# Attention and expert kernel on one core: last down groups reordered, gates by half rows, first half's results spread

## The reference, cut to what matters

```python
xn = _layernorm(x)
q, k, v = xn @ Wq.T + bq, xn @ Wk.T + bk, xn @ Wv.T + bv
phi_q, phi_k = elu(q) + 1, elu(k) + 1
s = (phi_q * cumsum(phi_k * v, axis=1) * SCALE) @ Wo.T + bo
h = gelu(buf @ w1.T + b1) @ w2.T + b2          # buf: the tokens in their slots
g = silu(gathered h * prob)
out = x + s * g
```

## Time and profile before

| | us |
|---|---|
| median of 3 runs | 2147.61 |
| lowest, highest | 2146.22, 2152.90 |
| the profiled execution's own time | 2152.81 |
| its span, first to last instruction | 2150.7 |
| PE busy | 2001.0 |
| DVE busy | 1380.1 |
| ACT busy | 687.4 |
| POOL busy | 471.6 |
| mean granted TensorE clock | 0.971 of full speed |

### The profile page before, as it was taken

The page is one execution under the profiler, slowest core; times in us unless marked ns, Lnnn a source line. Parts: engine busy times, 40 slices in busy tenths (PEclk is TensorE's granted clock), DMA queues, the critical chain, the costliest instruction groups (busy, mean ns, idle before and its releaser), DMA issues.

```text
span 2150.7 us, 27040 instructions
## 1 busy us (share of the span) xinstructions
PE 2001.0 (93%) x9380; PEld 910.8 (42%) x9380; DVE 1380.1 (64%) x2074; ACT 687.4 (32%) x1087; POOL 471.6 (22%) x577
## 2 busy tenths in 40 slices
PE   7799999999658999999999999989999999999993
PEld 2244454554223444444444443434444444444441
DVE  3587888778549766677667766476454544455453
ACT  1222222223335434443453343333122212221221
POOL 0078888888750000000000000110000000000002
PEclk9799999999879999999999999999999999999997
DMA  8566766667888776767676676874533333333334
GB/s 279 217 212 231 229 230 215 227 229 216 250 205 328 254 258 222 266 206 240 226 248 212 223 247 226 284 214 128 176 98 105 104 101 103 98 106 101 98 117 78
DMA packets 180278, 419.87 MB, mean 195 GB/s; under 512 B 17808, under 2 KB 74704, under 8 KB 178384
## 3 DMA queue, kind: packets, MB, share of 16 engines
q1 hardware_dynamic: 143728, 292.65, 41.9%
q0 software_dynamic: 29024, 117.51, 17.1%
q10 hardware_dynamic: 7424, 8.39, 1.3%
HBM read 268.51 MB, written 166.77 MB: 202 GB/s over the span
## 4 chain that ended last, share of the span: by engine, by line
PE 61%; POOL 13%; DMA 11%; DVE 6%; issue 4%; ACT 3%; another core or an unknown queue 1%; ACTq 0%; SPq 0%; DVEq 0%; POOLq 0%
PE pair L1761 33%; PE pair L1723 26%; DMA arena<-w_down 3%; DMA arena<-w_up 3%; DMA arena<-x_t 2%; PE pair L1577 2%; POOL arena L702 1%; POOL arena L704 1%; POOL arena L679 1%; POOL arena L691 1%; POOL arena L693 1%; POOL arena L695 1%; POOL arena L706 1%; POOL arena L696 1%; DMA arena<-up_sums 1%
## 5 line engine op out<-in xcount | busy, mean ns | idle before, releaser
L1761 PE MATMUL pair<-arena 128*128 128x512 f16 x3360 | 731.9, 380 | 7.7 <-DVE arena L1450 5.0
L1723 PE MATMUL pair<-xnT,arena 128*128 128x512 f16 x2400 | 537.4, 384 | 28.8 <-ACT arena L913 14.4
L1761 PEld LDWEIGHTS pair<-arena 128*128 128x128 f16 x3360 | 329.0, 98 | 407.7 <-issue 14.3
L1450 DVE SCALAR_TENSOR_TENSOR arena<-pair,arena 128x1024 f32<-128x1024 f32 x248 | 303.0, 1223 | 189.6 <-PE pair L1761 189.2
L1645 PE MATMUL pair<-arena 128*128 128x512 f16 x1728 | 385.9, 381 | 12.1 <-DVE xnT L423 12.1
L1723 PEld LDWEIGHTS pair<-xnT,arena 128*128 128x128 f16 x2400 | 236.5, 99 | 323.2 <-issue 20.7
L932 ACT ACTIVATE arena<-arena 128x512 f16<-128x512 f32 x280 | 170.2, 626 | 582.4 <-PE pair L1761 516.6
L1645 PEld LDWEIGHTS pair<-arena 128*128 128x128 f16 x1728 | 169.1, 98 | 208.6 <-issue 19.6
L1723 PE MATMUL pair<-xnT 128*128 128x512 f16 x960 | 216.6, 382 | 17.6 <-ACT xnT L863 17.6
L1426 DVE SCALAR_TENSOR_TENSOR arena<-arena 128x512 f16<-128x512 f32 x280 | 188.8, 683 | 10.9 <-ACT arena L932 9.1
L1723 PEld LDWEIGHTS pair<-xnT 128*128 128x128 f16 x960 | 94.4, 99 | 133.7 <-ACT xnT L863 18.6
(11 more groups left out here) (190 smaller groups left out, 1753.5 us busy)
## 6 DMA issues: line engine op xcount, KB each, us to landing
down_dram<-arena SPq DMA_DIRECT2D x70, 512.0 KB, 4.3
arena<-down_dram SPq DMA_DIRECT2D x70, 512.0 KB, 3.3
up_dram<-arena SPq DMA_DIRECT2D x100, 256.0 KB
arena<-up_dram SPq DMA_DIRECT2D x100, 256.0 KB, 2.6
arena<-w_up POOLq DMA_DIRECT2D x40, 512.0 KB, 5.3
up_sums<-arena POOLq DMA_DIRECT2D x40, 512.0 KB, 3.7
arena<-w_down POOLq DMA_DIRECT2D x40, 512.0 KB, 5.2
down_sums<-arena POOLq DMA_DIRECT2D x40, 512.0 KB, 3.6
```

What stands on the lines that cost most here:

```text
L1450: ins = nc.vector.scalar_tensor_tensor(to, src, scale, to, ALU.mult, ALU.add)
L1723: ins = mm(out_to, w[:, a, c * P:(c + 1) * P], x_in_op[:, b, c, :], start=(first and i == 0), stop=(i == 11), skip_group_check=True)
L1761: ins = mm(bank[2 + h][:, (t % 2) * BLOCK:(t % 2 + 1) * BLOCK], g_ops[:, A_NAMES.index(name), c, a, t * P:(t + 1) * P], down_ring[:, j, c, ...
```

## The change

LAST is the second half's last down group (n = 19). There PE does the tiles in two passes: all seven products for tiles 0 and 1, then all seven for tiles 2 and 3. DVE adds each tile by itself (`last_add`, 128x512), and PE waits before each tile for the last add to the same bank half. ACT gates each block of a tile by itself (`last_gate`, 128x512) in the order LAST_GATES, C11, C12, C22, C21 for the tiles of a pass. The results are made in the order 0, 1, 4, 5, 2, 3, 6, 7 within the down group, between adds, and POOL stores them in that order (LAST_TILES). In both halves' last down group only S3, S2 and the low part of S2 stand ahead of the first add; S4, S1 and the other low parts follow between the adds. The first half's results are spread: in quads 20 and 21 one is made after `p167`, one after `c22`, one after `c21` and one after `context(k, 3)`.

```diff
@@ -397,6 +397,18 @@
             return k // 2 - 1, (4, 5, 6) if 0 < k < 2 * GROUPS else ()
         VALUES = ("11", "22", "12", "21")
+        LAST = STEPS - 1
+        def last_at(j, t):
+            return 14 * LAST + 14 * (t // 2) + 2 * j + t % 2
+        LAST_INTO = {C11: 1, C12: 4, C22: 5, C21: 6}
+        LAST_GATES = [(c, 2 * h + t) for h in range(2) for c in (C11, C12, C22, C21) for t in range(2)]
+        LAST_TILES = (0, 1, 4, 5, 2, 3, 6, 7)
         def chain_bank(k):
             return out_bank(k % 2)
@@ -747,7 +759,7 @@
             def add_rows(half, i):
                 st = HALF_TILES * half + i
-                pool.wait_ge(fin_ready, st + 1)
+                pool.wait_ge(fin_ready, HALF_TILES + LAST_TILES.index(i) + 1 if half else i + 1)
                 pool.indirect_dma_start(
                     out, bass.IndirectOffsetOnAxis(ap=meta_s[:, st, 0:1].bitcast(U32), axis=0), fs(i, half), None,
                     bounds_check=TOKENS - 1, oob_is_err=False, compute_op=ALU.add).then_inc(fin_stored[i % PAIRS], 16)
@@ -757,7 +769,7 @@
             for half in range(HALVES):
                 if half:
                     save_s(GROUPS + ATT_GROUPS - 1)
-                for i in range(HALF_TILES):
+                for i in LAST_TILES if half else range(HALF_TILES):
                     add_rows(half, i)
             for i in range(PAIRS):
                 pool.wait_ge(fin_stored[i], 64)
@@ -932,13 +944,17 @@
                 nc.scalar.activation(g_ops[:, A_NAMES.index(name), k % 2, HI, :], g_block(name), ACT.Copy,
                                      scale=CS if is_attention(n) else HS).then_inc(g_hi, 1)
-            def gate(half, i):
-                st = HALF_TILES * half + i
+            def gate(i):
                 act.wait_ge(meta_loaded, 16)
-                act.wait_ge(down_added, 14 * (GROUPS * (half + 1) - 1) + (14 if i >= PAIRS else 10))
+                act.wait_ge(down_added, 14 * (GROUPS - 1) + (14 if i >= PAIRS else 10))
                 row = acc[:, i % PAIRS, 2 * (i // PAIRS):2 * (i // PAIRS) + 2, :].rearrange("p c e -> p (c e)")
-                nc.scalar.activation(row, row, ACT.Silu, scale=meta_s[:, st, 1:2].bitcast(F32)).then_inc(gate_ready, 1)
+                nc.scalar.activation(row, row, ACT.Silu, scale=meta_s[:, i, 1:2].bitcast(F32)).then_inc(gate_ready, 1)
+            def last_gate(c, t):
+                st = HALF_TILES + PAIRS * (c // 2) + t
+                act.wait_ge(down_added, last_at(LAST_INTO[c], t) + 1)
+                nc.scalar.activation(acc[:, t, c, :], acc[:, t, c, :], ACT.Silu, scale=meta_s[:, st, 1:2].bitcast(F32))\
+                  .then_inc(gate_ready, 1)
             def gate_weights():
                 act.wait_ge(scaled, 1)
...
-                gate(1, i)
+            for c, t in LAST_GATES:
+                last_gate(c, t)
@@ -1450,9 +1466,19 @@
                     ins = nc.vector.scalar_tensor_tensor(to, src, scale, to, ALU.mult, ALU.add)
                 ins.then_inc(down_added, 1)
+            def last_add(j, t):
+                dve.wait_ge(down_done, 14 * LAST + last_at(j, t) + 1)
+                dve.wait_ge(down_added, last_at(j, t) - 1 if j else 14 * LAST)
+                to = acc[:, t, DOWN_INTO[j], :]
+                nc.vector.scalar_tensor_tensor(to, bank[2 + t // 2][:, (t % 2) * BLOCK:(t % 2 + 1) * BLOCK], 1.0 / (HS * WM),
+                                               to, ALU.mult, ALU.add).then_inc(down_added, 1)
             def result(half, i):
-                st = HALF_TILES * half + i
-                dve.wait_ge(gate_ready, st + 1)
+                if half:
+                    dve.wait_ge(gate_ready, HALF_TILES + LAST_GATES.index((C21 if i >= PAIRS else C12, i % PAIRS)) + 1)
+                else:
+                    dve.wait_ge(gate_ready, i + 1)
                 dve.wait_ge(fs_loaded[i], 16 * (half + 1))
                 row = acc[:, i % PAIRS, 2 * (i // PAIRS):2 * (i // PAIRS) + 2, :].rearrange("p c e -> p (c e)")
                 nc.vector.tensor_tensor(fs(i, half), fs(i, half), row, ALU.mult).then_inc(fin_ready, 1)
...
                 p167(k)
-                if half and k in (2 * GROUPS, 2 * GROUPS + 1):
-                    for i in range(PAIRS):
-                        result(0, i + PAIRS * (k % 2))
+                finishing = half and k in (2 * GROUPS, 2 * GROUPS + 1)
+                if finishing:
+                    result(0, PAIRS * (k % 2))
                 if ups:
                     low_up(k + 1, 2)
                 for j in downs[:-3]:
...
                 c22(k)
+                if finishing:
+                    result(0, PAIRS * (k % 2) + 1)
                 for j in downs[-3:-2]:
                     low_down(m, j)
                 context(k, 1)
                 if ups:
                     low_up(k + 1, 4)
                 c21(k)
+                if finishing:
+                    result(0, PAIRS * (k % 2) + 2)
                 if in_line(k):
                     low_g(k, "22")
                 for j in downs[-2:-1]:
...
                 context(k, 3)
+                if finishing:
+                    result(0, PAIRS * (k % 2) + 3)
                 if in_line(k):
                     low_g(k, "12")
                 for j in downs[-1:]:
@@ -1516,14 +1548,6 @@
                 last = n % GROUPS == GROUPS - 1
                 k = 2 * n + 2
                 ups = half == 0 and not last
-                if last:
-                    e = 2 * n + 1
-                    s3(e)
-                    s2(e)
-                    s4(e)
-                    s1(e)
-                    for name in ("S2", "S1", "S4", "S3"):
-                        low_g(e, name)
                 for j in range(7):
                     add_down(n, j, 0)
                     if j and not last:
@@ -1535,15 +1559,35 @@
                     if j == 0 and not last:
                         s3(k)
                         s2(k)
-                    if last and j == 6 and half:
-                        for i in range(PAIRS):
-                            result(half, i)
                     if ups:
                         low_up(2 * n + 3, j)
                         for i in downs_under(n).get(j, ()):
                             low_down(n + 1, i)
                 if not last:
                     low_g(k, DOWN_A[6])
+            def last_down(n):
+                half, e = n // GROUPS, 2 * n + 1
+                s3(e)
+                s2(e)
+                low_g(e, "S2")
+                for at in range(14):
+                    if half:
+                        j, h = at % 7, at // 7
+                        last_add(j, 2 * h)
+                        last_add(j, 2 * h + 1)
+                    else:
+                        j, h = at // 2, at % 2
+                        add_down(n, j, h)
+                    if at == 0:
+                        s4(e)
+                        s1(e)
+                    elif at < 4:
+                        low_g(e, ("S1", "S4", "S3")[at - 1])
+                    if half:
+                        for i in {5: (0,), 6: (1,), 7: (4,), 8: (5,), 11: (2,), 12: (3,), 13: (6, 7)}.get(at, ()):
+                            result(half, i)
             for half in range(HALVES):
                 n0 = half * GROUPS
...
                 for n in range(n0, n0 + GROUPS):
                     if n < n0 + GROUPS - 1:
                         quad(2 * n + 2)
-                    down(n)
-                    if n < n0 + GROUPS - 1:
+                        down(n)
                         quad(2 * n + 3)
-            for i in range(PAIRS, HALF_TILES):
-                result(1, i)
+                    else:
+                        last_down(n)
@@ -1746,23 +1789,35 @@
                 pe.wait_ge(copy_ready, 3 * k + 3)
                 product(k, 6, chain, False)
+            def down_tile(n, j, t):
+                i = 0
+                for c in range(2):
+                    for a, b in PASSES:
+                        ins = mm(bank[2 + t // 2][:, (t % 2) * BLOCK:(t % 2 + 1) * BLOCK],
+                                 g_ops[:, A_NAMES.index(DOWN_A[j]), c, a, t * P:(t + 1) * P], down_ring[:, j, c, b, :],
+                                 start=(DOWN_STARTS[j] and i == 0), stop=(i == 5), skip_group_check=True)
+                        i += 1
+                ins.then_inc(down_done, 1)
             def down(n):
                 for j in range(7):
-                    name = DOWN_A[j]
                     pe.wait_ge(down_w[j], 16 * (n + 1))
-                    pe.wait_ge(g_lo, made_count(2 * n + 1, name))
+                    pe.wait_ge(g_lo, made_count(2 * n + 1, DOWN_A[j]))
                     for t in range(PAIRS):
-                        h, e = t // 2, 14 * n + 2 * j + t // 2
+                        e = 14 * n + 2 * j + t // 2
                         if t % 2 == 0 and e >= 2:
                             pe.wait_ge(down_added, e - 1)
-                        i = 0
-                        for c in range(2):
```

(20 more changed lines are left out.)

7 lines of the change are left out of this document (3 added, 4 removed).

## The result

| | before | changed |
|---|---|---|
| median, us | 2147.53 (4 runs, 2146.22 to 2152.90) | 2122.99 (4 runs, 2119.28 to 2131.61) |
| ratio | | 0.9890, 95% interval 0.9862 to 0.9918 |
| profiled execution, us | 2152.81 | 2131.61 |
| its span, us | 2150.7 | 2129.8 |

The change saves 24.5 us by the medians, where 32.9 were forecast. The prediction said 2115 us, with a range of 2107 to 2128; the measured 2123 lies in it. Each of the two profiled executions is the slowest of its four.

The account below looks back on a forecast made before the run. Bounds: PE, busy 93% of the span, and 35.7 us behind the last matmul, bound by transfers. Savings 5.4 + 10 + 0.3 - 0.6 + 17.8 = 32.9 us gave 2115 us from the median, range 2107 to 2128.

Parts of the forecast that it names:

- rival 1: Quads' feed (kv rows, s_dram rows, SP's late up loads) replaces the results as limit: 3 instead of 10 us, 2122; chance 0.2.
- The tail: Behind the last matmul: most stores move beside matmuls, span ends 17.9 us after it instead of 35.7, 17.8 saved.
- the quads: Quads 20 to 22: spreading the first half's results removes idle and slow starts, about 10 us saved, bounds 3 and 13.
- First half's last down group: Only S2's low half stays ahead of the first add: idle 0.9 instead of 3.36 us, 5.4 saved in all.
- the slow start: First half's last down group: 14 matmuls behind the idle at 0.427 instead of 0.216 us, 2.95 us counted as saved.
- The steps up to quad 21's fifth product: Quad 20 onward: 0.9 us idle left of 4.16, fifth product at 1402.4 instead of 1407.2, 4.8 us gained.
- Margin 3 to 5 us less a landing of about 4: this may cost 0 to 3: Quad 22's first product: SP issues up loads only after rows 4 to 7; possible cost 0 to 3 us, within bounds.
- two of the prediction's own signs of being wrong: Quads 21 and 22: SP's up loads releasing PE or DVE waits over 2 us; granted clock of 0.50.
- Second half's last down group: Two passes of tiles: idle 1.35 instead of 1.65 us, 0.3 saved, less 0.6 for the turns.
- the turns: Second half's last down group: each tile added while PE does the other, 0.4 us spare; cost 0.6 us, bounds 0 and 2.
- Rivals 2 and 3: Second half's last down: turns cost 8.4 us, 2122.5, chance 0.07; matmuls blocked by DVE reading the bank pair, 2174, chance 0.03.
- Rival 4: Tail: first tiles' stores wait until the second pass is over, about 9 of 17.8 us lost, 2124; chance 0.05.

Follow-up runs that it names:

- e4: Changed kernel with all four sums and four low parts again ahead of the first add in the first half's last down group: 2126.79 us.
- e6: The kernel before the change, run and profiled again without any edit: 2128.71 us, ratio 0.9997 to the runs beside it.
- e2: Changed kernel with quad 22's up operands 0 to 3 each loaded ahead of the wait for store 0 to 3: 2120.01 us.
- e8: e2 with the first half's results 4 to 7 made later, 4 behind quad 21's C21, 5 to 7 in quad 22: 2098.00 us.
- e3: Changed kernel with the second half's last down group by pairs of tiles again, all results behind the last add: 33.8 us behind the last matmul.
- e10: The changed kernel again, unedited, timed beside the kernel before: 2109.03 us against 2133.34, ratio 0.9891.
- e1: Changed kernel with the first half's results again in a row behind P1+P6+P7 in quads 20 and 21: 2128.71 us.
- e9: e8 with GpSimd's 32 scatters issued after the first down group: 2088.53 us against 2133.34 for the kernel before, ratio 0.9794.
- e7: Changed kernel with GpSimd's 32 scatters issued after the first down group: 2098.13 us against 2127.72 for the kernel before, ratio 0.9860.

## Why the prediction was right, and where it was not

The forecast saving was 32.9 us, the measured one 24.5, and rival 1's number, 2122, is nearer to 2123 than the forecast's 2115. The tail was forecast well; the quads were not, and the number lies in the range because the range takes in rival 1.

*First half's last down group.* 0.9 us of idle was forecast, 0.83 measured; the 5.4 us are (a) before less (a) after. But 2.95 of these are the slow start, and this was read from one execution as if it were steady. e4 and e6 have the same idle without it. Against those two this edit saves 2.5 us.

*Quads.* The steps up to quad 21's fifth product hold: idle 0.9 forecast, 0.76 measured; at that product 1402.4 was forecast, 4.8 gained, and 7.3 measured (from C11 of quad 20, 32.0 against 24.7), since context 3 did not wait for its kv rows at all: they are issued 3.4 us earlier after C11 than before (10.3 against 13.7) and are there within 7.1 us instead of 12.0. That stop is not steady either: e6, with its results in a row, has none. The round-robin rule (the Trainium skill, DMA: Bandwidth & Descriptors, section SWDGE vs HWDGE vs iDMA) was drawn on for rival 1: a kv load would not get shorter as long as any store is in flight. The trace does not bear out what was drawn from it, since two stores were issued around this load (1386.79 and 1389.01).

The step that failed is "Margin 3 to 5 us less a landing of about 4: this may cost 0 to 3". SP was free 31.0 us after quad 20's C11 (before 30.5), as forecast. But PE came to quad 22's first product at 32.7, where 34.8 was forecast and 39.8 measured before, so the margin was 1.7 us, not 3 to 5; and the landing took 8.2 us, not 4. The cost was 6.7 us of idle and 2.8 of slow start. So the quads gave 4.6 instead of 10. I had the right wait in the sum, with a price near the 3.8 us of the same load in the kernel before (5.1 in e6), and no fall of the clock behind it. In the kernel before no store was issued between 1391.30 and 1412.36; in the changed one a store goes out at 1406.65, 1.2 us before this load, and it took 8.2, 8.0 and 9.3 us in the three traces of the changed kernel. The other six up loads also follow it more closely here (within 5.1 us against 10.1), so which of the two made it slow is not shown. e2 shows the cause of the wait, and e8 what lay behind it. Rival 1 named SP's late up loads, and two of the prediction's own signs of being wrong are in the trace, an up load that releases PE after more than 2 us and a clock of 0.50 behind it: here the rival took place.

*Second half's last down group.* Forecast: idle 1.35 instead of 1.65 and 0.6 for the turns, +0.3 in all; measured: idle 1.18, (d) 38.3 against 38.2. The turns cost about 0.8 us (38.3 less 36.3 of matmuls and 1.2 of idle). Rivals 2 and 3 are out: 156 matmuls in 34.37 us, 0.220 each. What I did not see is that the sums' new places alone would have taken all idle there (e3).

*Tail.* T + 17.9 forecast, T + 17.8 measured; before T + 35.7, so 17.9 saved against the first profile and 16.4 against e6. Last store at T + 4.8 forecast, 4.7 measured. The store landed 6.6 us later, at T + 11.3, where 11.8 was forecast, and from there to the end are 6.5 us, not 6.1: two small misses that offset each other. Rival 4 is out. The Trainium skill, VectorE: DVE Perf Modes, section The TRN2 errata — SBUF-src ops pay a fixed extra latency per instruction, says that many small tiles pay the SBUF latency once each. The trace agrees in that two half adds take 1.38 us and a whole one 1.22; which latency that is, no run shows. The page's advice is tiles of 512 elements or more, which a half add has, so it speaks less against the edit than the prediction took it to.

*Sum.* By the two profiles 27.9 against 32.9, and the gap is in the quads (4.6 instead of 10). The medians say 24.5, 20.3 and 24.3. Against e6's stages the change saves 19.6 (changed kernel) or 16.8 (e10's). So the sum was made against a profiled execution that was long in the very stages it priced: it has 2.9 us more than e6 in (a), the fall of the clock, 3.9 more in (b), the stop at the fifth product and longer slow starts, and 1.5 more in (e). What makes the stretch ahead of the start differ by some 10 us between executions is open.

## What to carry to other kernels

A stretch of stores behind the last matmul is worth ordering the last matmuls for: finish some output tiles early, even if each hand-over gets smaller. When work is spread over a stage, follow the queue that waits for it in order (here SP's) to the next load behind it, and price that load by landings measured beside other transfers that will run then. And read one stage from two executions before a term of the sum rests on the clock.

## What the hardware showed that I had not expected

In these traces the length of TensorE's idle did not tell, between 1.97 and 3.70 us, whether its granted clock would fall. Behind the 3.36 to 3.37 us of the first half's last down group it fell to 1.2 GHz in one of three executions and stayed at 2.4 GHz in two. At the last product of quad 5, in code that no edit touches, PE is idle for 2.25 to 3.07 us in all thirteen traces, and the 12 matmuls behind take 2.76 us in six of them and 4.08 to 4.45 in seven. The two with the same idle are e1, where the clock fell, and e9, where it did not:

```profile
814.30 4.36 PE L1761 MATMUL pair<-xnT 128*128 128x512 f16 x12 [2.25 <-ACT xnT L875]
816.00:818.00 2.00, 2.00 (x6) 0.65 (x5) 1.47 (x3) 2.00 (x4) 0.00 (x0) 0.50 0.04 15
...
788.54 2.76 PE L1768 MATMUL pair<-xnT 128*128 128x512 f16 x12 [2.25 <-ACT xnT L877]
790.00:792.00 2.00, 2.00 (x11) 0.88 (x9) 1.23 (x3) 2.00 (x4) 0.00 (x0) 1.00 0.07 25
```

From 590 us on, the shortest idle with a fall behind it was 1.97 us (e2, 36 matmuls in 9.63 us) and the longest without one 3.70 (e7, 36 in 7.94). Behind 4.16 us and more it fell each time, for a time that differed. So the prediction's reading, full rate behind 1.99 us and half rate behind 3.36 and more, held for the trace it was made from and not for the next ones.

The load of the same 256 KB landed in 3.8 and 5.1 us in the two traces of the kernel before and in 8.0 to 9.3 in the three of the changed one, where an indirect adding store had been issued 1.2 to 1.4 us ahead of it. While GpSimd issued 32 small scatters, PE, DVE and ACT stood still for 13 us and more with the DMA engines idle in the changed kernel's trace, and far less on the second chip; issued later, they cost 9.5 us less there. The kernel before had a median 11 to 17 us lower in the two groups of runs on the second chip than in the one on the first.
